# Graph attention layers on one core: the step from phase A to phase B reordered, and the padding edges' table rows

## The reference

```python
for l in range(3):
    f1 = relu(x[row] @ nb_W[l] + nb_b[l])
    f2 = relu(x[col] @ self_W[l] + self_b[l])
    h = relu(concatenate([f1, f2], axis=1) @ att1_W[l] + att1_b[l])
    log_alpha = (h @ att2_W[l] + att2_b[l])[:, 0]
    mask = clip(sigmoid(log_alpha) * (ZETA - GAMMA) + GAMMA, 0.0, 1.0)
    rowsum = segment_sum(mask, row, num_segments=n) + 1e-06
    d_inv_sqrt = clip(rowsum ** (-0.5), 0.0, 10.0)
    vals = mask * d_inv_sqrt[row] * d_inv_sqrt[col]
    x = segment_sum(vals[:, None] * x[col], row, num_segments=n)
    out = out + x
```

## Time and profile before

| | |
|---|---|
| median of three runs | 9865.02 us (9862.49 to 9868.52) |
| the profiled execution, its own time | 9852.52 us |
| its span, first to last instruction | 9850.6 us |
| mean granted TensorE clock | 0.639 of full speed |
| busy: PE, DVE, ACT, POOL | 6201.2, 7410.5, 2922.9, 6194.6 us |

### The profile page before, as it was taken

How to read it: one execution, slowest core, us unless ns; L and a number is a source line. 1 busy time by engine, 2 the same in 40 slices (tenths; PEclk the granted TensorE clock), 3 DMA queues, 4 the chain that set the end, 5 groups by cost and what they waited for, 6 DMA issues and landing times.

```text
span 9850.6 us, 206958 instructions
## 1 busy us (share of the span) xinstructions
PE 6201.2 (63%) x44403; PEld 5462.9 (55%) x44722; DVE 7410.5 (75%) x29659; ACT 2922.9 (30%) x7919; POOL 6194.6 (63%) x6324
## 2 busy tenths in 40 slices
PE   3145555555569986555555549997555555556997
PEld 1135455455458875454554548886555545555886
DVE  8867777777768886777777768886777777776888
ACT  0021111111137772111111117774111111114776
POOL 0017777777755545777777765554777777775553
PEclk7565555555569996555555559998555555557998
DMA  0012222233254442222232254443222222326444
GB/s 21 0 42 71 71 71 72 71 71 72 71 94 119 118 113 67 71 72 71 71 72 71 71 65 125 118 119 82 72 71 71 71 71 71 72 71 100 118 118 99
DMA packets 921874, 778.05 MB, mean 79 GB/s; under 512 B 697300, under 2 KB 700660, under 8 KB 921460
## 3 DMA queue, kind: packets, MB, share of 16 engines
q0 software_dynamic: 199680, 368.45, 18.2%
q1 hardware_dynamic: 722164, 409.31, 15.2%
HBM read 620.19 MB, written 157.08 MB: 79 GB/s over the span
## 4 chain that ended last, share of the span: by engine, by line
PE 28%; POOL 25%; issue 19%; DVE 14%; ACT 8%; DMA 7%; ACTq 1%; DVEq 0%; POOLq 0%; SPq 0%
POOL k_hot L435 11%; PE bank L461 10%; POOL got L435 10%; PE bank L534 6%; PE bank L566 6%; DMA got<-qx_table,index 4%; POOL g_hot L435 4%; ACT p_all L671 3%; DVE acc L796 2%; DVE acc L797 2%; PE bank L571 2%; ACT onehot_t L686 2%; ACT p_all L682 2%; DMA k_hot<-qx_table,index 1%; PE bank L524 1%
## 5 line engine op out<-in xcount | busy, mean ns | idle before, releaser
L534 PE MATMUL bank<-p_all,onehot_t 128*128 x10032 | 2301.4, 424 | 1628.7 <-issue 1619.1
L534 PEld LDWEIGHTS bank<-p_all,onehot_t 128*128 128x128 f32 x10032 | 2186.7, 330 | 1679.7 <-issue 1679.7
L435 POOL DMA_INDIRECT got<-qx_table,index x2496 | 2391.5, 958 | 798.5 <-issue 758.6
L448 POOL DMA_INDIRECT got<-y_table,index x1248 | 1354.3, 1085 | 1163.7 <-ACT index L704 653.7
L653 ACT ACTIVATE small<-small 128x8 f32<-128x8 f32 x624 | 130.2, 209 | 5101.7 <-DVE small L920 5101.7
L461 PE MATMUL bank<-mask,onehots 128*128 128x3 bf16 x4992 | 676.4, 184 | 1265.8 <-DVE mask L931 1265.8
L435 POOL DMA_INDIRECT g_hot<-qx_table,index x1248 | 1199.4, 961 | 380.3 <-issue 377.6
L435 POOL DMA_INDIRECT k_hot<-qx_table,index x1248 | 1198.6, 960 | 380.3 <-issue 364.8
L461 PEld LDWEIGHTS bank<-mask,onehots 128*128 128x128 bf16 x4992 | 519.3, 104 | 1536.0 <-issue 1428.8
L967 DVE SCALAR_TENSOR_TENSOR p_all<-iota_b,col_hi,bank 128x104 f32<-128x104 bf16 x3768 | 952.1, 315 | 290.0 <-PE bank L566 289.9
L896 DVE TENSOR_SCALAR onehots<-iota_b,rows_now 128x128 bf16<-128x128 bf16 x5040 | 917.0, 289 | 22.5
(11 more groups left out here) (160 smaller groups left out, 9901.6 us busy)
## 6 DMA issues: line engine op xcount, KB each, us to landing
p_all<-col_rows SPq DMA_DIRECT2D x474, 256.0 KB, 3.7
kept_x<-got SPq DMA_DIRECT2D x312, 256.0 KB
k_x<-kept_x SPq DMA_DIRECT2D x312, 256.0 KB
got<-qx_table,index POOLq DMA_INDIRECT x2496
kept_x<-g_hot SPq DMA_DIRECT2D x156, 256.0 KB
p_all<-kept_x SPq DMA_DIRECT2D x156, 256.0 KB
g_hot<-qx_table,index POOLq DMA_INDIRECT x1248
k_hot<-qx_table,index POOLq DMA_INDIRECT x1248
```

What stands on the lines that cost most here:

```text
L435: pool.indirect_dma_start(got[j][:, k, :], None, qx_table, bass.IndirectOffsetOnAxis(ap=index[j][:, k:k + 1], axis=0)).then_inc(a_got[j], 16)
L448: pool.indirect_dma_start(got[j][:, k, 0:HID], None, y_table, bass.IndirectOffsetOnAxis(ap=index[j][:, k:k + 1], axis=0)).then_inc(g_got[j ...
L534: last = mm(bank_p[h][:, k, :], onehot_t[h][:, k, :], p_all[:, ds(ids[k], 1), :].rearrange("p o d -> p (o d)"), start=True, stop=True)
```

## The change

It has two parts.

**The seam.** DVE makes the `d3` parts directly after `d_node`, then the first one-hot `look_onehot(0, 0)`, and only then `y`, in eight pieces of 13 blocks, each with its own `m_y`. SP no longer waits for `y` before it loads the first two blocks of columns: it waits until PE has read `p_all` for the last time in A (`a_p`), loads them, and then stores each piece of `y` as it comes. POOL and the layer's end wait for the eight stores together.

**The padding keys.** `LAST_KEY` and the padding keys of the blocks get the partition's number as their column: a per-partition `last_key` takes the place of the constant, and `pad_keys` is or-ed with `part_i`.

```diff
-    LAST_VALUE = struct.unpack("f", struct.pack("i", LAST_KEY))[0]
...
-                sp.wait_ge(m_y, l + 1)
-                sp.dma_start(y_table.rearrange("(p b) d -> p b d", p=PARTS), x_cur[:, :, :]).then_inc(m_yst, 16)
+
+                sp.wait_ge(a_p, (l + 1) * (GROUPS + 1))
+                sp.wait_ge(t_table, 16)
+                sp.sem_inc(sp_go, 1)
+                for i in range(2):
+                    load_columns(i, i * U)
+                for c in range(PIECES):
+                    sp.wait_ge(m_y, l * PIECES + (c + 1))
+                    sp.dma_start(y_table.rearrange("(p b) d -> p b d", p=PARTS)[:, piece(c), :],
+                                 x_cur[:, piece(c), :]).then_inc(m_yst, 16)
                 for j in range(3):
                     sp.wait_ge(a_kept[j], (l + 1) * (16 * QUADS))
                     sp.sem_inc(sp_go, 1)
...
-                sp.wait_ge(t_table, 16)
-                for i in range(2):
-                    load_columns(i, i * U)
-                sp.sem_inc(sp_go, 1)
...
-                pool.wait_ge(m_yst, (l + 1) * 16)
+                pool.wait_ge(m_yst, (l + 1) * (16 * PIECES))
...
-            v.memset(keys[0][:, ECOLS + BLOCKS:COLS].bitcast(I32), LAST_KEY)
...
+            v.tensor_scalar(last_key[:, :].bitcast(I32), part_i[:, :], LAST_KEY, None, ALU.bitwise_or)
...
+            v.tensor_tensor(pad_keys.bitcast(I32), pad_keys.bitcast(I32), part_i[:, :].to_broadcast([PARTS, BLOCKS]),
+                            ALU.bitwise_or)
+            v.tensor_copy(keys[0][:, ECOLS + BLOCKS:COLS], last_key[:, :].to_broadcast([PARTS, COLS - ECOLS - BLOCKS]))
...
-            link(v.tensor_scalar(unused, bank[7][:, 0:BLOCKS], part_f[:, :], LAST_VALUE, ALU.is_le, ALU.mult))
+            link(v.tensor_scalar(unused, bank[7][:, 0:BLOCKS], part_f[:, :], last_key[:, :], ALU.is_le, ALU.mult))
...
-                v.tensor_tensor(x_cur[:, :, :], x_cur[:, :, :], d_wide, ALU.mult).then_inc(m_y, 1)
                 link(v.tensor_copy(d3[:, 0, :], d_node[:, :]), e)
...
                 look_onehot(0, 0)
+                for c in range(PIECES):
+                    some = piece(c)
+                    v.tensor_tensor(x_cur[:, some, :], x_cur[:, some, :], d_wide[:, some, :], ALU.mult).then_inc(m_y, 1)
                 look_up(0, 0, 0)
                 weigh(0, 0, 0)
```

More of the change, by code:

```diff
@@ L18 @@
 import math
-import struct
 from contextlib import ExitStack
@@ L138, in build @@
         part_f = sb("part_f", [PARTS, 1], F32)
+        last_key = sb("last_key", [PARTS, 1], F32)
         ident_b = sb("ident_b", [PARTS, PARTS], BF16)
@@ L365, in _, with load_columns @@
                         sp.dma_start(qx_rows[:, ds((b * 2 + h) * GRP, GRP), 0:HID], q_step[h][:, :, :]).then_inc(n_qst[h], 16)
+                def load_columns(c, at):
+                    sp.dma_start(k_cols[c], col_rows[ds(at, U), :].rearrange("t e -> (t e)")
+                                 .partition_broadcast(PARTS).rearrange("p (t e) -> p t e", e=PARTS)).then_inc(k_colin[c], 16)
                 with sp.Fori(0, QUADS) as b:
@@ L377, in _ @@
                     sp.sem_inc(sp_go, 1)
-                def load_columns(c, at):
-                    sp.dma_start(k_cols[c], col_rows[ds(at, U), :].rearrange("t e -> (t e)")
-                                 .partition_broadcast(PARTS).rearrange("p (t e) -> p t e", e=PARTS)).then_inc(k_colin[c], 16)
-                sp.wait_ge(t_table, 16)
-                for i in range(2):
-                    load_columns(i, i * U)
-                sp.sem_inc(sp_go, 1)
                 with sp.Fori(0, B_BODIES) as b:
@@ L1023, in _ @@
                 dve.wait_ge(k_rows, (l + 1) * (2 * (K_STEPS + 2)))
-                dve.wait_ge(m_yst, (l + 1) * 16)
+                dve.wait_ge(m_yst, (l + 1) * (16 * PIECES))
                 v.tensor_tensor(x_cur[:, :, :], acc[:, 0:NB, :], d_wide, ALU.mult).then_inc(l_end, 1)
```

## The result

| | before | after |
|---|---|---|
| median of 6 runs | 9865.23 us (9862.49 to 9868.52) | 9780.7 us (9776.31 to 9782.32) |
| the profiled execution | 9852.52 us | 9776.31 us |

The ratio is 0.9914 (95% interval 0.9904 to 0.9923): faster by 84.5 us, where 66 were forecast. The forecast of 9799 is 18 us too high; the time lies in its range of 9779 to 9854, but only 1.7 us above the low end.

The account below looks back on a forecast made before the run. Phase A was taken as paced by POOL's gather issues and, in its tail, by same-row DMA transfers; the seam by y's store. 3 x (18 tail + 4 seam) = 66 us gave 9799 us, range 9779 to 9854.

Parts of the forecast that it names:

- The tail: End of phase A: gathers of padding rows overlap once they read 17 rows; 18 us a layer, bounds 0 and 23.3.
- The price worked out for a gather of one row: Tail of A: 52 gathers read table row 0 128 times each, taking about 1.70 us against POOL's 1.26 us issue.
- (a): Tail of A: the last tiles stay slow, only the seam's 12 us gained, 9853 us; chance 0.18.
- (b): Tail of A: only two-row tiles overlap, 14.4 us a layer or less, 9810 to 9838 us; chance 0.20.
- The seam up to POOL: Between A and B: y stored in pieces lets POOL's first gather start at D+14.3, 4.4 us earlier.
- the prediction's D: The seam's reference time, when `d_node` is there: 2833.89 in the kernel before.
- The 24 us in a row: Seam: by the skill page's formula, eight piece stores of 3.0 us each, one after another.
- rival (d): SP's queue at the seam: pieces stored one after another, +12.3 us a layer, with (a) 9902 us; chance 0.05.
- The `k` path: Seam: look-up at D+9.2 instead of D+21.3, ACT's first scaling about D+14 instead of D+24.9.
- the clock: Start of B: PE's pause for `g` can delay its clock rise, by at most half of the 5 us at 0.55.
- rival (c): Tail and seam: full relief and full PE gain, 3 x (23.3 + 6.8) = 90 us, 9775 us; (c) or near it 0.07.
- the 9799 of the likeliest case: Whole kernel: 18 us from the tail and 4 from the seam a layer, 66 us in all; chance 0.50 for 9781 to 9811.

Follow-up runs that it names:

- Runs of 1 tile: Kernel after with padding keys laid so the 52 last tiles hold one row each, a new row every tile: 12541.54 us, old kernel there 12541.41.
- runs of 1 and 4: Kernel after with one row per last tile, the row changing every tile (12541.54 us) or every fourth tile (12509.67 us; old kernel there 12525.37).
- the first four experiments: On one quick chip: seam with old padding keys 9866.87 us, new padding keys with old seam 9804.77, kernel after with lane-own rows 9780.96, kernel before again 9884.82.
- the padding keys alone: Kernel before with only the new padding keys, seam unchanged: 9804.77 us, ratio 0.9919 to the kernel before on the same chip.
- the seam alone: Kernel after with the padding keys of the kernel before: 9866.87 us beside 9885.77 for the kernel before on that chip, ratio 0.9981.

## Why the prediction was right

**The tail: right in kind, under-sized.** The forecast was 18 a layer, between bounds of 0 and 23.3; measured are 22.4 (and 25.5 on the chip where the tail was longer). The price worked out for a gather of one row, 1.70 us, stands: the tail's delay of 29.6 on the other chip would make it 1.26 + 27.0 / 52 = 1.78. What failed in size is the choice between the ends. The forecast let the engines separate mainly in tiles of two rows and kept 5 us back for those of one. Runs of 1 tile show that no two-row tile is needed. It was enough that the tail's work fell under POOL's pace: at 170 us for a megabyte a gather costs the engines 0.7 us, where POOL issues one each 1.26, and the delay is nearly the steady one. The prediction was right that the rows must overlap and that they do.

**Rivals (a) and (b)** fell with it: (a), no overlap, asked for a tail as long as before; (b), overlap in two-row tiles only, for 14.4 a layer at most, and runs of 1 and 4, which have no such tiles, were both relieved. The blocks' own paddings were forecast at 0, and on the chip of the first four experiments the gathers before the tail take the same with the old and the new ones. What the forecast missed is that the last gathers of B read single rows too: 1.9 us a layer in "the padding keys alone", 0.4 on the first chip.

**The seam up to POOL: right.** Counted from the prediction's D (2815.93 here), 14.3 was forecast and 14.5 is measured in layer 0, 13.9 in the mean; `y` is complete at D+8.9 for 9.2; the gain is 4.8 for 4.4. It rested on eight stores overlapping, and they do: first issue at 2818.35, last landing before 2830.46, 12.1 us for 3.4 MB that came piecemeal from 7.6 us of DVE work. The formula of the Trainium skill (DMA: Bandwidth & Descriptors, "Anatomy of one DMA") gave 3.0 us for such a store alone. The page measured it for DMAs that GpSimd issues, and these are SP's; the trace's median of 2.9 agrees all the same. The 24 us in a row, and with them rival (d), did not come. The 1 MiB of its "Bandwidth" section is advice about a rate, and here a store's rate mattered less than its start: with one store of 3.4 MB the path is 6.2 us longer.

**The `k` path: too optimistic, and it cost nothing.** Forecast for ACT's first scaling was D+14, measured is D+17.5. The step overlooked: ACT runs in order, and ahead of the scaling stands its one-hot of the third step, whose columns are a third load, queued behind the eight stores (issued at 2826.49; ACT idle for 13.94 us until it landed). ACT still waited 5.10 us for `g` afterwards, where 8 were forecast. That wait is the cover, and it held. The 8 were off in more than this delay: ACT's `g` batch came at D+26.5 and not at D+28.3, and ACT's work between was 3.9 us, where the forecast leaves some 6.

**The start of B: a cost forecast that wasn't one.** 0.4 a layer was kept for the clock. The granted clock was 0.56 from 2838 to 2843, with PE busy all 5 us, and 1.00 after that: it rose about 27 us after D, where in the kernel before it was 34. PE took `g` at D+29.2 (forecast 29.5). From POOL's first gather to ACT's scaling it is 1.2 us shorter. In layer 0 POOL's issues are most of this: in the kernel before, three of the eight gathers took 1.96, 1.75 and 1.51 us instead of 0.94, in the kernel after one took 1.50. In layer 2 they are not, and what shortened it there no run shows. B after ACT's first `g` is 1.0 shorter in these two traces, 0.4 of it by the padding rows at its end; with the seam alone it isn't shorter (802.5 beside 802.3). So the seam gave 5.9 by itself on one chip and at most 6.6 on the other, in place of 4.

Together: 3 x (22.4 + 7.0) = 88 against 3 x (18 + 4) = 66, and 84.5 in the medians. The tail's share of this is three quarters; of the forecast's 22 it was four fifths. The time lies nearer to rival (c), full relief and full gain at the seam for 9775, than to the 9799 of the likeliest case: the tail came out near its bound of 23.3, and the 7.0 of seam and B lie just above theirs of 6.8. Both terms were too small; with a little more in either, the time would have left the range. (c) had been given 0.07, too little. The chances as listed make 0.77 for faster by more and 0.18 for within, not 0.76 and 0.19, which changes nothing.

**Setup:** forecast 0; the first addition of the layers starts at 614.0 instead of 614.7 us.

## What to carry to other kernels

Ask of every gather how many different rows its descriptors name: padding that all points at row 0 can make the last tiles of a sorted list the slowest ones, with DVE and ACT mostly idle and the DMA share near 1 while few bytes move. Sorting undoes a spread that is put into the keys, so spread after the sort, or be sure that a partial spread brings the work under the pace of what issues it. At a seam, cut a dependent store into pieces that leave while the rest is being made, and count which loads queue behind them on the same engine.

## What the runs showed of the hardware

- **128 reads of one 512-byte row** take some 1.7 us a gather when the neighbouring gathers read the same row. The DMA queue then needs 364 us of an engine for a megabyte where it needs 66 in the steady stretch of the same trace; on the slow chips it is 395 against 65 and 376 against 58. With a new row in each tile it is 146.
- **Chips differ.** The same kernel took 9865, 9886 and 9852 us on three chips (the record does not name the first; that it is one of its own is inferred from its time) and 12,541 and 12,525 (one run) on two others, where engines stood idle with nothing in the profile that ended it, and where the end of A was mostly bound by something else. A ratio of one chip says little about another: the kernel after gains 0.86% on the first and 0.17% on a slow one.
- **One long-running pace varies.** POOL's 1,600 gathers of a layer took 2022.8 us in one execution and 2027.3 in another of the same kernel on another chip: 13 us over three layers, as much as the whole seam of this change was forecast to give. Whether the chip or the execution makes it is open.
- **A gather's issue on POOL** takes 0.94 us, and up to 1.93 beside DVE in phase B. In the kernel after, POOL's third gather of B, which starts at 2832.98, takes 1.50 us, and DVE's one-hot of 0.48 us starts within it at 2833.58. The Trainium skill (SBUF — State Buffer, "Who interferes with whom") has DVE and GpSimd share one pair of ports, which one holds for a whole instruction while the other waits; the 0.55 us that are too many here agree with the 0.48 of DVE's instruction. The page lets the one that issues first go first. That is not seen here: POOL's instruction began first, and it is the one that grew.
